# Mixture-of-experts layer with random-feature attention on one core: gate and up weights in 4 KB runs, transposes two experts ahead, a 320-column first gate product, gathers one expert earlier

## The reference

```python
xn = layernorm(x)                                  # no weight, no bias
# 1. attention through 512 random features
feats   = AB/sqrt(512) * exp(xn @ (ab*proj).T - 0.5*sum(xn*xn)*ab*ab)
weights = the same of input_weights
attn    = feats @ weights.T
# 2. mixture of experts, E = 64 experts, I = 256, 8 per token, at most CAP = 256 tokens each
scores  = sigmoid(xn @ router_w)                   # best 4 of 8 groups of experts, then 8 experts
w       = 2.5 * scores of the 8 / their sum
for e in experts:                                  # tokens in order, the first 256 of each expert
    h = silu(rows @ gate_w[e]) * (rows @ up_w[e])
    out[token] += w * (h @ down_w[e])
out += (silu(xn @ sgate) * (xn @ sup)) @ sdown     # a shared expert for every token
return x + attn + out
```

## Time and profile before

| | us |
|---|---|
| median of 3 runs | 1309.34 (1308.23 to 1309.87) |
| the profiled execution, its own time | 1307.97 |
| its span in the trace | 1306.2 |
| PE busy | 1280.0 (98%) |
| DVE busy | 916.0 (70%) |
| ACT busy | 647.3 (50%) |
| POOL busy | 433.9 (33%) |
| share of PE in the chain that ended last | 96% |

### The profile page before, as it was taken

One profiled execution on the slowest core, in us unless ns is written; L12 is line 12 of the kernel. 1 busy time (PEld: TensorE's weight loads), 2 busy tenths in 40 slices (PEclk: granted clock), 3 DMA queues, 4 the chain that ended last, 5 costly groups with the idle time before them and its releaser, 6 DMA issues.

```text
span 1306.2 us, 22561 instructions
## 1 busy us (share of the span) xinstructions
PE 1280.0 (98%) x7565; PEld 1123.8 (86%) x7565; DVE 916.0 (70%) x1787; ACT 647.3 (50%) x1053; POOL 433.9 (33%) x344
## 2 busy tenths in 40 slices
PE   6999999999999999999999999999999999999995
PEld 5888888888888888888889999999999999999994
DVE  7878877777777777785656667667766766676662
ACT  4421232212322123221256777777877777777772
POOL 1000000000000000000014666777666667676653
PEclk9999999999999999999999999999999999999998
DMA  7336554664546645445447999999999999999995
GB/s 269 121 107 163 130 121 127 157 166 98 130 119 153 167 104 131 114 118 134 134 133 214 286 278 286 287 290 292 290 291 285 298 291 287 282 295 285 298 277 65
DMA packets 203800, 263.65 MB, mean 202 GB/s; under 512 B 49268, under 2 KB 138744, under 8 KB 203768
## 3 DMA queue, kind: packets, MB, share of 16 engines
q1 hardware_dynamic: 175096, 191.93, 50.9%
q0 software_dynamic: 28672, 71.32, 23.7%
HBM read 178.18 MB, written 71.39 MB: 191 GB/s over the span
## 4 chain that ended last, share of the span: by engine, by line
PE 96%; DVE 2%; DMA 1%; ACT 0%; issue 0%; POOL 0%; SPq 0%; ACTq 0%
PE pmm L1255 18%; PE pmm L1257 18%; PE pmm L1256 18%; PE pout L1255 11%; PE pout L1257 11%; PE pout L1256 11%; PE ptr L1488 4%; PE plog L1316 2%; PE plog L1325 1%; PE ptr L1267 0%; DMA out_dram<-outs,slot_cols 0%; DVE stats L829 0%; DMA xbuf<-_L_attn_proj_matrix_dram 0%; DVE xt_lo L795 0%; PE plog L1345 0%
## 5 line engine op out<-in xcount | busy, mean ns | idle before, releaser
L1614 POOL DMA_INDIRECT out_dram<-outs,slot_cols x128 | 228.7, 1787 | 165.6 <-DMA out_dram<-outs,slot_cols 136.2
L1255 PE MATMUL pmm<-xt_hi,proj_hi 128*128 128x256 f32 (+1 forms) x784 | 253.0, 323 | 2.2 <-DVE xt_lo L795 1.4
L1257 PE MATMUL pmm<-xt_hi,proj_lo 128*128 128x256 f32 (+1 forms) x784 | 249.6, 318 | 0.0
L1256 PE MATMUL pmm<-xt_lo,proj_hi 128*128 128x256 f32 (+1 forms) x784 | 249.6, 318 | 0.0
L1255 PE MATMUL pmm<-xt_hi,sgu_hi 128*128 128x256 f32 (+1 forms) x768 | 246.1, 320 | 0.2 <-issue 0.2
L1256 PE MATMUL pmm<-xt_lo,sgu_hi 128*128 128x256 f32 (+1 forms) x768 | 243.4, 317 | 0.0
L1257 PE MATMUL pmm<-xt_hi,sgu_lo 128*128 128x256 f32 (+1 forms) x768 | 243.4, 317 | 0.0
L1598 POOL TENSOR_TENSOR earlier<-earlier,chosen 128x64 bf16<-128x64 bf16 x64 | 23.9, 373 | 617.8 <-DVE chosen L916 614.0
L1604 POOL DMA_INDIRECT xbuf<-rows,slot_cols x128 | 175.3, 1369 | 80.8 <-issue 38.6
L552 ACT ACTIVATE feat<-pmm,ab 128x512 f32<-128x512 f32 x68 | 46.7, 687 | 292.4 <-PE pmm L1257 286.4
L1255 PEld LDWEIGHTS pmm<-xt_hi,proj_hi 128*128 128x128 f32 x784 | 147.3, 188 | 13.6 <-ACT feat L552 1.6
(11 more groups left out here) (185 smaller groups left out, 2543.7 us busy)
## 6 DMA issues: line engine op xcount, KB each, us to landing
raw<-in_L_ffn_gate_w_dram SPq DMA_DIRECT2D x64, 512.0 KB
raw<-in_L_ffn_up_w_dram SPq DMA_DIRECT2D x64, 512.0 KB
raw<-in_L_ffn_down_w_dram SPq DMA_DIRECT2D x64, 512.0 KB
outs<-in_L_attn_x_dram SPq DMA_DIRECT2D x32, 512.0 KB, 3.9
out_dram<-outs SPq DMA_DIRECT2D x32, 512.0 KB, 3.0
xbuf<-in_L_attn_x_dram SPq DMA_DIRECT2D x52, 256.0 KB, 7.6
raw<-xn SPq DMA_DIRECT2D x52, 256.0 KB, 6.2
rows<-raw SPq DMA_DIRECT2D x39, 256.0 KB, 4.2
```

Of the source, the lines that this page charges most:

```text
L1255: pe.matmul(psum, lh, rh, start=first and n == 0, stop=False)
L1256: pe.matmul(psum, lh, rl, start=False, stop=False)
L1257: ins = pe.matmul(psum, ll, rh, start=False, stop=final and n == len(pairs) - 1)
L1614: pool.indirect_dma_start(out=out, out_offset=bass.IndirectOffsetOnAxis(ap=slot_cols[:, at:at + 1], axis=0), in_=outs[e.b][:, c, :], in_of ...
```

## The change

Four things are changed.

1. **Weights.** `load_half` loads gate and up with partition p taking rows 4p to 4p+3, one run of 4 KB instead of four of 1 KB. So the contraction index of the gathered rows must be in the same order, and the row table is written with permuted columns. A new `copy_rows(g)` on ACT makes that copy (four instructions of 128x512 and two small ones a group) into parts of `raw` that are free then, and SP's `store_rows` writes it (two DMAs for each of the first three groups, eight for the others). They replace `store_xn` and `store_xn_quads`. `normalise` of the next group waits for `rows_copied`. In SP's queue the store stands behind `store_w`, not ahead of `store_counts`. `copy_rows` stands at the end of a group on ACT, but at other places for the first three groups.
2. **Order of stage 2.** The transposes are made two experts ahead and between gate_up and down: PE's turn is gate_up(e), e_turn(e+2), down(e-1). ACT: gate_up_hi(e+1), silu(e), down_hi(e), turned_hi(e+2), hidden_hi(e), e_out(e-1). DVE: gate_up_lo(e+1), down_lo(e), hidden(e), turned_lo(e+2), hidden_lo(e); `slot_tokens` moves to the start of its turn.
3. **First gate product.** The first product of an expert reads 320 columns instead of 256. The 64 more are written to a part of `pmm` that the following products start anew.
4. **POOL.** gather(n) is followed by add_rows(n-5), not add_rows(n-4).

```diff
+E_LEAD = 64
 # SP
                 sp.dma_start(raw[b][:, at].rearrange("p (c i) -> p c i", c=HB),
-                             weights.rearrange("(c p) i -> p c i", p=P)).then_inc(gu_loaded[b][m], 16)
+                             weights.rearrange("(p c) i -> p c i", p=P)).then_inc(gu_loaded[b][m], 16)
...
+            def store_rows(g):
+                sp.wait_ge(rows_copied, 2 * (g.n + 1))
+                for a in range(2):
+                    at = slice(2 * a, 2 * a + 2)
+                    if isinstance(g.n, int) and g.n < STD:
+                        sp.dma_start(rows_groups[g.n][:, at, 0:H], row_place(g, a)).then_inc(
+                            rows_stored, 16)
+                    else:
+                        for q in range(P // SQ):
+                            sp.dma_start(rows_quads[g.n, q][:, at, 0:H], row_place(g, a)[q:P:P // SQ]).then_inc(
+                                rows_stored, 16)
...
-                store_xn_quads(later)
                 store_counts(g)
                 store_out(g, 0)
                 store_w(nxt)
+                store_rows(later)
                 store_out(g, 1)
 # ACT
+            def copy_rows(g):
+                act.wait_ge(norm_made, g.n + 1)
...
+                    for i in range(2):
+                        j = 2 * a + i
+                        to = row_place(g, a)[:, i]
+                        if std:
+                            ins = act.activation(to.rearrange("p (c q) -> p c q", c=HB),
+                                                 xn[:, j].rearrange("p (q c) -> p c q", c=HB), copy)
...
+                    act.activation(row_place(g, a)[:, :, 0], xn_first[:, 2 * a:2 * a + 2], copy).then_inc(rows_copied, 1)
...
                 hi_half(2, half, xt_hi[0], (pout2, ptr)[half])
+            copy_rows(turn(0))
             features(0, 3, wt_hi, scale=ab2[:, 3:4])
...
             def stage(e, next_rows=True, next_weights=True, out_prev=True, look=None):
-                if next_rows:
-                    e_turned_hi(e.next())
                 if next_weights:
                     gate_up_hi(e.next())
                 e_silu(e)
                 down_hi(e)
+                if next_rows:
+                    e_turned_hi(e.next().next())
                 e_hidden_hi(e)
 # DVE
-                if next_rows:
-                    e_turned_lo(e.next())
+                if tokens is not None:
+                    slot_tokens(tokens)
                 if next_weights:
                     gate_up_lo(e.next())
+                down_lo(e)
                 e_hidden(e)
-                down_lo(e)
+                if next_rows:
+                    e_turned_lo(e.next().next())
                 e_hidden_lo(e)
 # PE, e_gate_up
+                        lead = m == 0 and i == 0
+                        if lead:
+                            pe.matmul(pmm[m][:, 0:CAP + E_LEAD], egu_hi[e.b][:, at[0]],
+                                      xt_hi[e.b][:, 0, E_COLS.start:E_COLS.stop + E_LEAD], start=True, stop=False)
 # PE, the loop
-                    e_turn(e.next())
                     e_gate_up(e)
                     if k == 1:
                         look_up(m + 2)
+                    e_turn(e.next().next())
                     e_down(e.prev())
 # POOL
-                if n >= 4:
-                    add_rows(turn(n - 4))
+                if n >= 5:
+                    add_rows(turn(n - 5))
```

More of the change, by code:

```diff
@@ L434, in first_group @@
                 load_residual(g)
+                store_rows(nxt)
+                load_x_quads(turn(3))
                 store_w(g)
@@ L495, in _ @@
             sp.wait_ge(iw_sums_turned, 1)
-            store_xn(turn(0))
+            store_rows(turn(0))
             load_x(turn(2))
@@ L617, in first_group @@
                 hidden(g, 0)
+                copy_rows(nxt)
                 hidden_hi(g, 0)
@@ L636, in second_group @@
                 exp_logits(nxt)
+                copy_rows(Turn(g.i + 1, g.b))
             def gate_up_hi(e, parts=(0, 1)):
@@ L643, in gate_up_hi, with group @@
                                    egu_raw[e.b][:, at], copy).then_inc(egu_hi_made[m], 1)
-            def group(g, last=False):
+            def group(g, last=False, copies=True):
                 nxt = g.next()
@@ L669, in group @@
                     exp_logits(nxt)
+                if copies:
+                    copy_rows(Turn(g.i + 1, g.b))
             act.wait_ge(ab_made, 1)
@@ L709, in _ @@
                     group(Turn(i, b))
-            group(turn(GROUPS - 2))
-            group(turn(GROUPS - 1), last=True)
+            group(turn(GROUPS - 2), copies=False)
+            group(turn(GROUPS - 1), last=True, copies=False)
             def down_hi(e):
@@ L753, in _ @@
             e_turned_hi(turn(0))
+            e_turned_hi(turn(1))
             stage(turn(0), next_weights=False, out_prev=False)
@@ L761, in _ @@
             for n in range(E - 6, E - 1):
-                stage(turn(n))
+                stage(turn(n), next_rows=n < E - 2)
             stage(turn(E - 1), next_rows=False, next_weights=False)
@@ L1242, in _ @@
                 for k in range(CHUNK):
-                    stage(four(2 * m + 1, k), look=(pass_blocks, None, slot_tokens, None)[k] and (
-                        (pass_blocks, None, slot_tokens, None)[k], m + 2))
+                    stage(four(2 * m + 1, k), tokens=m + 2 if k == 2 else None, blocks=m + 2 if k == 0 else None)
             for n in range(E - 6, E - 1):
-                stage(turn(n))
+                stage(turn(n), next_rows=n < E - 2)
             stage(turn(E - 1), next_rows=False, next_weights=False)
@@ L1251, in _, with products @@
         def _(pe):
-            def products(psum, pairs, first=True, final=True):
+            def products(psum, pairs, first=True, final=True, lead=False):
                 for n, (lh, ll, rh, rl) in enumerate(pairs):
-                    pe.matmul(psum, lh, rh, start=first and n == 0, stop=False)
+                    if n > 0 or not lead:
+                        pe.matmul(psum, lh, rh, start=first and n == 0, stop=False)
                     pe.matmul(psum, lh, rl, start=False, stop=False)
@@ L1499, in e_gate_up @@
                               for h in range(HB)]
+                        lead = m == 0 and i == 0
+                        if lead:
+                            pe.matmul(pmm[m][:, 0:CAP + E_LEAD], egu_hi[e.b][:, at[0]],
+                                      xt_hi[e.b][:, 0, E_COLS.start:E_COLS.stop + E_LEAD], start=True, stop=False)
                         ins = products(pmm[m][:, i * CAP:(i + 1) * CAP], [
                             (egu_hi[e.b][:, at[h]], egu_lo[e.b][:, at[h]], xt_hi[e.b][:, h, E_COLS],
-                             xt_lo[e.b][:, h, E_COLS]) for h in range(HB)])
+                             xt_lo[e.b][:, h, E_COLS]) for h in range(HB)], lead=lead)
                     ins.then_inc((e_gate_done, e_up_done)[m], 1)
@@ L1522, in _ @@
             e_gate_up(turn(1))
+            e_turn(turn(3))
             e_down(turn(0))
@@ L1627, in _ @@
                 gather(turn(n))
-                if n == 3:
+                if n == 4:
                     for b in range(2):
                         pool.wait_ge(out_stored[b], 16 * GROUPS)
-                if n >= 4:
-                    add_rows(turn(n - 4))
-            for n in range(E - 4, E):
+                if n >= 5:
+                    add_rows(turn(n - 5))
+            for n in range(E - 5, E):
                 add_rows(turn(n))
```

71 lines of the change are left out of this document (38 added, 33 removed).

## The result

The changed kernel takes 1322.01 us (median of 4 runs, 1319.95 to 1324.67), beside 1309.33 for the kernel before (4 runs). The ratio is 1.0095, with an interval of 1.0069 to 1.0121. It is 12.7 us slower, where 1303.4 was forecast. The profiled execution took 1319.95 us, with a span of 1317.9 us, against 1306.2 before.

The account below looks back on a forecast made before the run. PE was taken as the bound, its time being instruction count by pace. The terms -10.2 - 1.3 + 2.0 + 2.8 + 0.8 = -5.9 us gave 1302.1 profiled, 1303.4 median; the 8-in-10 range was 1298.5 to 1313.5, the forecast's own 1299 to 1307.

Parts of the forecast that it names:

- the one on POOL: POOL's adds in stage 2: one more expert between gather and add delays nothing PE waits for; nothing, while 2.0 us lasts.
- the prologue: First group's `copy_rows` on ACT: some 3.1 us of copies, of which 0.8 us reaches PE, between 0 and 1.5.
- the pace: Gate and up products: the 320-column first product makes some 60 slow experts fast, turns 9.10 instead of 9.27, -10.2 us.
- DMA or POOL: Rival for stage 2: DMA or POOL gives the gain back, the turn stays 9.27, +1.5 us, 1310.8; chance 0.10.
- The look-ups: Moved transposes in the 14 turns with a look-up: one break between product lengths serves both, 14 x 0.09 = -1.3 us.
- The start of stage 2: DVE splits the first expert's down weights ahead of `hid`, so the second expert's gate products wait: +2.0 us, 1.0 to 2.1.
- The turn behind a look-up: DVE's swapped steps make `hid` late where ACT is late; PE waits 0.2 us in 14 turns, +2.8 us, 0 to +8.4.
- 4 KB runs: Weight loads: shorter transfers give nothing themselves, since PE doesn't wait for weights; they only make room.

Follow-up runs that it names:

- e5: Changed kernel with odd experts' adds sent to a second table in DRAM, their part missing from the output; 1304.53 us, ratio 0.9954 to the kernel before.
- e2: Changed kernel without the 64 extra columns, so the first gate product has 256 columns; 1328.32 us, ratio 1.0137 to the kernel before.
- e3: Changed kernel with `hid` ahead of the split of the down weights on DVE again, in all turns; 1323.62 us, ratio 1.0117 to the kernel before.
- e10: Changed kernel with the old order of stage 2, no 64 columns, and the first group's copies in two halves; 1311.95 us, ratio 1.0021 to the kernel before.
- e7: Kernel before with the 320-column first gate product alone; 1309.58 us, ratio 0.9990 to the kernel before.
- e6: Changed kernel loading only half of each expert's down weights from the third expert on, the other half being old data; 1315.36 us, ratio 1.0037 to the kernel before.

## Why the prediction was wrong

**The step that failed** is the one on POOL: "POOL waits 113.7 us for its adds over 57 turns, 2.0 a turn [...] Nothing, as long as that 2.0 lasts". I read the 2.0 us as room, since POOL was idle then. It was the contrary: the wait is a part of the chain, the landing of the last pair of adds. The room of a serial chain is what it waits for its input, here ACT's output, and the same answer showed none of that. I should have taken the round from the timeline, add to add, which is 9.4 us before with no such wait in it, and set it beside the turn I forecast, (3 x 9.10 + 9.6)/4 = 9.2. PE can't run faster than that chain for 64 turns: ACT stands still when its two output buffers are full. The term was put at nothing. In the trace after it is 12.3 us: 6.8 in the turns (9.1 of waits, less the 2.3 that e5 has without the chain) and 5.5 at the end. Forecast and measured span are 17.6 us apart (-5.9 and +11.7); the prologue has 3.8 of the rest, the pace 1.8. The rival "DMA or POOL" was the right one, with 0.10, but I bounded it at 9.27 a turn and gave it nothing at the start and the end. It costs there too. The first pairs start late (the fifth expert's first add at 759.4, against 746.8 before). The chain doesn't catch up, since it takes 9.38 a turn. In the end its last pair starts at 1307.1, against 1295.8:

```profile
1292.09 1.55 POOL L1661 DMA_INDIRECT out_dram<-outs,slot_cols  x1 [4.20 <-DMA out_dram<-outs,slot_cols]
...
1299.55 1.55 POOL L1661 DMA_INDIRECT out_dram<-outs,slot_cols  x1 [4.05 <-DMA out_dram<-outs,slot_cols]
...
1307.11 1.55 POOL L1661 DMA_INDIRECT out_dram<-outs,slot_cols  x1 [4.14 <-DMA out_dram<-outs,slot_cols]
```

**The pace** (-10.2) was right in kind: all experts that PE enters without waiting run fast. Ordinary turns are 9.13, not 9.10: the products behind the long one need some five gaps to come down from 118 to 113 ns, which is half of the 0.03, and the fast turns of e2 are 9.09 where they were 9.07 before, so the moved transposes cost the other half. That makes 0.14 a turn, some -8.4 us. The cause that the prediction gave, a weight load that stands two slots ahead or one, doesn't hold. With loads and products paired by their order, a load starts 0.22 us ahead of the first gate product in the 118 ns experts of e2 as in the 113 ns experts of the kernel after, and from the tenth product on it is one slot ahead in both, 0.115 and 0.110. So this term came true partly by luck.

**The look-ups** (-1.3): 0.46 a look-up instead of 0.54, 14 times, -1.1. Right.

**The start of stage 2** (+2.0): +2.0, and gone in e3. Right.

**The turn behind a look-up** (+2.8): in e5, where the chain doesn't disturb it, it comes to 2.3 us. The size was right, its form was not. PE stands at most 0.02 us ahead of the gate products, where 0.1 to 0.3 was forecast; what is lost is 0.08 in the first gaps behind, and 0.19 more in the five experts that then go at the slow pace. What the kernel after shows on top is the late ACT.

**The prologue** (+0.8) came out at +2.1 without the fall of the clock and +3.7 with it; the other 0.9 of the +4.6 are the spread of the start. A copy that gathers every fourth value took 1.07 us, where I had taken the 0.63 of a plain one from the earlier trace rows; the sum was 4.5, not 3.1. DVE's cushion of 0.7 was used up and 2.1 us reached PE. And I had not thought of the clock, which took 1.6 more in the profiled execution of after.

**4 KB runs**: packets fell from 203800 to 126488, and the time that the queue's packets took from 50.9% to 47.7% of the span. It bought nothing that was seen (e10).

The Trainium skill, "TensorE: Matmul & The Clock Gate", section "Back-to-back issue gap", would have given one pace for 256 columns. e2 and the kernel after differ in 64 columns of one product per expert, and in 118 against 113 ns for most of the 46 behind it, so the rule is not enough here. For a product at the lower clock it gives N/1.2 ns, 427 for 512 columns. With that the trace agrees (48.48 to 48.91).

## What to carry to other kernels

A wait of an engine for its own earlier transfers is no slack: add up one round of such a chain, from start to start, take off what it waits for its input, and compare it with the turn that is hoped for. A kernel that is 98% one engine can have a second bound within 1% of it, and then a faster first engine only makes buffers full, wherever the order leaves least room. Work that is put into a cover of idle time should be cut to the size of each gap, and a strided copy priced by a strided copy.

## What the runs showed of the hardware

- A stream of 256-column products with a weight load each has two paces at the same clock, 113 and 118 ns. It was fast where gate followed 512 columns with a first product of 320 and no wait (48 of 48 experts after), and slow without the 64 columns (e2, 56 of 63) and behind transposes (e7, 61 of 63). Where PE entered from a wait or just in time it was slow in 8 of 15 experts after. What sets the pace was not shown.
- Behind a pair of indirect adds of 128 rows of 2 KB each, the next that depends on it started 5.5 us on average after the end of the last issue, beside full DMA traffic and with two gathers issued in between. At the end of the kernel, with nothing beside it, it started 4.1 us after. With a tenth less traffic (e6) the round fell from 9.38 to 9.29, which is PE's mean turn there, so it may have been able to fall further.
- Behind a gap of 2.4 us in the prologue PE's clock fell to the 1.2 GHz level in three of six profiled executions. The first slow product started 0.6 to 1.2 us after the gap, and seven or eight were slow.
- ACT's copy of 128x512 values that takes every fourth took 1.07 us, against 0.63 for the nearest plain row.
